# Transformer layers on one NeuronCore: one block per layer instead of three or four, attention started on chunk 0, stack loads on SyncE's queue

## What is computed

```python
x = x + attn_a(layernorm(x))      # gated cumulative attention, once
x = x + ffn(layernorm(x))         # two layers, below
x = x + attn_b(layernorm(x))      # softmax attention, 16 heads of 8, not causal
x = x + ffn(layernorm(x))         # the same two layers again
# ffn: for l in 0, 1:
#   x = x + attn(ln(x)) @ wo + bo                     causal softmax attention, 16 heads of 8
#   h = ln(x)
#   x = x + (token_moe if l == 0 else seq_moe)(h)     top 2 of 8 experts, per token or per sequence
```

## Time and profile before

| | before |
|---|---|
| median of 3 runs | 3304.18 us (3303.13 to 3309.66) |
| the profiled execution | 3296.16 us |
| its span, first to last instruction | 3294.4 us |
| TensorE clock granted, mean | 0.900 of full speed |
| busy: PE, DVE, ACT, POOL | 81%, 78%, 69%, 16% |

### The profile page before, as it was taken

One profiled execution on the slowest core, in us unless ns is written; L12 is line 12 of the kernel. 1 busy time (PEld: TensorE's weight loads), 2 busy tenths in 40 slices (PEclk: granted clock), 3 DMA queues, 4 the chain that ended last, 5 costly groups with the idle time before them and its releaser, 6 DMA issues. The chain is left out here.

```text
span 3294.4 us, 71887 instructions
## 1 busy us (share of the span) xinstructions
PE 2673.7 (81%) x28144; PEld 1180.8 (36%) x28144; DVE 2570.5 (78%) x3323; ACT 2276.4 (69%) x4368; POOL 533.6 (16%) x1036
## 2 busy tenths in 40 slices
PE   4459999599499994759999999289996996699976
PEld 3322332488233332512222222133332784223325
DVE  5659998577498994769999997489995675699956
ACT  1137898377278984539999999168885674488965
POOL 3023110244131001100000000022101342221001
PEclk8669999799599997869999999689997898799988
DMA  1060000121500001140000000510001112300010
GB/s 31 4 146 29 13 10 10 59 60 42 128 21 13 12 10 45 40 90 8 8 10 8 10 8 8 142 34 15 12 10 51 52 49 75 80 16 12 10 37 26
DMA packets 114079, 119.06 MB, mean 36 GB/s; under 512 B 15063, under 2 KB 94733, under 8 KB 113741
## 3 DMA queue, kind: packets, MB, share of 16 engines
q1 hardware_dynamic: 96460, 96.63, 11.1%
q10 hardware_dynamic: 16640, 15.73, 1.9%
q0 software_dynamic: 640, 2.10, 0.3%
HBM read 70.31 MB, written 43.78 MB: 35 GB/s over the span
## 5 line engine op out<-in xcount | busy, mean ns | idle before, releaser
L1185 ACT ACTIVATE h_probsf<-h_ps_scoresf 128x512 f32<-128x512 f32 (+3 forms) x1216 | 603.5, 552 | 157.0 <-PE h_ps_scoresf L1137 144.5
L1185 ACT ACTIVATE h_probsg<-h_ps_scoresg 128x512 f32<-128x512 f32 (+3 forms) x1216 | 603.6, 552 | 151.3 <-PE h_ps_scoresg L1137 138.9
L1185 ACT ACTIVATE h_probsb<-h_ps_scoresb 128x512 f32<-128x512 f32 x1024 | 556.3, 596 | 73.5 <-PE h_ps_scoresb L1137 63.4
L1159 PE MATMUL h_ps_valuesf<-h_probsf,v_all 128*9 128x256 f32 (+2 forms) x4608 | 349.4, 375 | 29.3 <-POOL h_probsf L1248 21.7
L1159 PE MATMUL h_ps_valuesg<-h_probsg,v_all 128*9 128x256 f32 (+2 forms) x4608 | 348.8, 375 | 26.0 <-POOL h_probsg L1248 18.5
L1159 PE MATMUL h_ps_valuesb<-h_probsb,v_all 128*9 128x256 f32 x4096 | 318.4, 383 | 9.4 <-ACT h_drainedb L1192 4.2
L1208 DVE TENSOR_REDUCE h_maxima_0b<-h_ps_scanb 128x2 f32<-128x1024 f32 x256 | 292.5, 1216 | 10.8 <-PE h_ps_scanb L1099 9.9
L1208 DVE TENSOR_REDUCE h_maxima_2b<-h_ps_scanb 128x2 f32<-128x1024 f32 x256 | 292.8, 1217 | 6.7 <-PE h_ps_scanb L1099 6.7
L1208 DVE TENSOR_REDUCE h_maxima_0f<-h_ps_scanf 128x2 f32<-128x1024 f32 x224 | 259.2, 1219 | 22.4 <-PE h_ps_scanf L1099 22.2
L1099 PE MATMUL h_ps_scanf<-k_stack,q_stack 48*128 48x512 bf16 (+3 forms) x1280 | 218.6, 364 | 70.5 <-DVE h_ps_valuesf L1197 51.1
L1099 PE MATMUL h_ps_scang<-k_stack,q_stack 48*128 48x512 bf16 (+3 forms) x1280 | 217.2, 362 | 71.3 <-DVE h_ps_valuesg L1197 51.3
(11 more groups left out here) (404 smaller groups left out, 4287.0 us busy)
## 6 DMA issues: line engine op xcount, KB each, us to landing
q_stack<-combine_weights SPq DMA_DIRECT2D x64, 256.0 KB, 3.2
q_stack<-in_L_ffn_e_w SPq DMA_DIRECT2D x24, 256.0 KB, 2.8
q_stack<-q_parts ACTq DMA_DIRECT2D x20, 256.0 KB, 8.4
k_stack<-k_parts ACTq DMA_DIRECT2D x20, 256.0 KB, 9.9
q_stack<-q_parts SPq DMA_DIRECT2D x20, 256.0 KB, 8.7
k_stack<-k_parts SPq DMA_DIRECT2D x20, 256.0 KB, 10.6
attended<-h_drainedf SPq DMA_DIRECT2D x16, 256.0 KB, 2.2
attended<-h_drainedf SPq DMA_DIRECT2D x32, 128.0 KB, 1.9
```

The costliest lines, as they stand in the source:

```text
L1159: last = nc.tensor.matmul(ps_values[32 * j:32 * j + VD, low:high], m.v_all[:, kb, QUAD * quad + j, :], probs[:, (u + j % banks) % RING_P, ...
L1185: nc.scalar.activation(by_head(probs[:, of % RING_P, :], of), by_head(ps_scores[:, of % RING_S, :], of), ACT.Exp, scale=SOFTMAX_SCALE).the ...
```

## The change

One function, `layer`, now opens one block for a whole layer; the three or four functions write into it, so an engine goes from one to the next as soon as its own semaphores allow. The buffers of attention (`AttentionBuffers`) are allocated before the projection and freed before the experts. What the barriers ordered is now waited for: PE and DVE wait in attention for the projection's last uses of PSUM, SP's and POOL's part of `experts` waits for the end of `finish_attention`. The loads of the stacks move: ACT issues only chunk 0's half b = 1, in its turn for chunk 1 ahead of `copy_chunk(3)`; SP issues all the rest, chunk c - 1's after the high parts of chunk c. The semaphores are cleared at other places. Each block's body is otherwise the same.

```diff
@@ project_qkv: POOL, SP, ACT
-            m.clear_previous(pool)
+            m.clear(pool, "finish", "experts")
...
                     for k in range(2):
                         sp.wait_ge(ready, 2 * c + k + 1)
                         write_part(sp, c, k, part)
-                if c:
-                    load_stacks(sp, c - 1, 0)
+                    if c and part == 0:
+                        load_stacks(sp, c - 1, 0)
+                        if c > 1:
+                            load_stacks(sp, c - 1, 1)
             load_stacks(sp, CHUNKS - 1, 0)
+            load_stacks(sp, CHUNKS - 1, 1)
...
+                if c == 1:
+                    load_stacks(act, 0, 1)
                 if c + 2 < CHUNKS:
                     copy_chunk(c + 2)
...
-                if c:
-                    load_stacks(act, c - 1, 1)
-            load_stacks(act, CHUNKS - 1, 1)
+    return {"h": (h_ready, CHUNKS), "high": (high_ready, 2 * CHUNKS), "rest": (rest_ready, 2 * CHUNKS),
+            "v": (v_kept, CHUNKS)}
@@ attention_heads: PE, DVE, POOL
+            for done in ("h", "high", "rest", "v"):
+                pe.wait_ge(*projected[done])
             pe.wait_ge(cleared, 1)
...
+            dve.wait_ge(*projected["v"])
             nc.vector.memset(ps_values[:, :], 0.0).then_inc(cleared, 1)
...
-            m.clear_previous(pool)
@@ finish_attention
-        @block.gpsimd
-        def _(pool):
-            m.clear_previous(pool)
+        if layer is None:
+            @block.gpsimd
+            def _(pool):
+                pool.wait_ge(added, CHUNKS)
+                m.clear(pool, "project", "attention")
...
+                nc.vector.tensor_tensor(tiles, tiles, ps[:, c, :, :], ALU.add).then_inc(added, 1)
+                dve.wait_ge(added, c + 1)
+                last = chunk_stats(nc, m, dst, c)
+            last.then_inc(measured, 1)
+            dve.wait_ge(measured, 1)
...
+    return projected
@@ experts: POOL, SP
-            m.clear_previous(pool)
             inverse_root(nc, pool, m, m.rstd[:, :], tmp[:, 0, :], var_ready, rstd_ready, 1)
+            if by_token:
+                pool.wait_ge(hn_ready, CHUNKS)
             for e in range(n_exp):
                 pool.wait_ge(w2_in[e], 16)
...
                 pool.wait_ge(evacuated, y + 1)
+                if y == CLEAR_AT:
+                    m.clear(pool, "project", "attention", "finish")
...
+            sp.wait_ge(attended, CHUNKS)
             if by_token:
@@ new
+CLEAR_AT = 4
+def layer(nc, m, n, number=None, first=False, last=False, load_experts=False, out=None):
+    mixing = number is None
+    with nc.Block() as m.block, ExitStack() as ctx:
+        buffers = AttentionBuffers(nc, ctx, n, not mixing, load_experts)
+        projected = project_qkv(nc, m, n, first=first, layer=number)
+        attention_heads(nc, m, n, buffers, projected)
+        attended = finish_attention(nc, m, n, number)
+        ctx.close()
+        if not mixing:
+            experts(nc, m, n, number, last, attended, out)
```

More of the change, by code:

```diff
@@ L77, with phase_semaphores @@
 class Memory:
-    def phase_semaphores(self):
-        self.previous, self.current = self.current, []
+    def phase_semaphores(self, phase):
+        here = self.used[phase] = []
         def sem(name):
@@ L86, in sem, with clear @@
                 self.named[name] = self.ctx.enter_context(self.nc.semaphore(name))
-            self.current.append(self.named[name])
+            here.append(self.named[name])
             return self.named[name]
         return sem
-    def clear_previous(self, pool):
-        for s in self.previous:
-            pool.sem_clear(s)
+    def clear(self, pool, *phases):
+        for phase in phases:
+            for s in self.used.pop(phase, ()):
+                pool.sem_clear(s)
     def __init__(self, nc, ctx, ins):
-        self.nc, self.ctx, self.named, self.current, self.previous = nc, ctx, {}, [], []
+        self.nc, self.ctx, self.named, self.used, self.block = nc, ctx, {}, {}, None
         def sb(name, shape, dt=F32):
@@ L305, in chunk_stats @@
     for t in range(c * TPC, (c + 1) * TPC):
-        nc.vector.bn_stats(m.st[:, t, :], src[:, t, :])
+        last = nc.vector.bn_stats(m.st[:, t, :], src[:, t, :])
+    return last
 def token_stats(nc, step, m, tmp, var_ready, rstd_ready, count):
@@ L1049, in attention_heads @@
     with ExitStack() as ctx:
[L1050 to L1060, removed]
-        raw_weights = sb("h_raw_weights", [P, 2, FF]) if load_experts else None
+        sem = m.phase_semaphores("attention")
         ps_scan = ctx.enter_context(nc.psum_tensor("h_ps_scan" + n, [P, RING_A, 2, SCAN_KEYS], F32))
@@ L1070, in attention_heads @@
         out_done = [sem(f"h_out_done{k}") for k in range(2)]
-        block = ctx.enter_context(nc.Block())
+        block = m.block
         def by_head(bank, u):
@@ L1286, in sb @@
             return ctx.enter_context(nc.sbuf_tensor(name + n, shape, dt))
-        sem = m.phase_semaphores()
+        sem = m.phase_semaphores("finish")
         y = sb("f_y", [P, CHUNKS, CH])
@@ L1317, in _ @@
         def _(dve):
-            step = Steps(dve, dve_steps)
             dve.wait_ge(sums_in, 16)
@@ L1385, with experts @@
 CW_AT, TURN_BACK_AT = 8, 8
-def experts(nc, m, n, layer, last, out=None):
+CLEAR_AT = 4
+def experts(nc, m, n, layer, last, attended, out=None):
     by_token = layer == 0
@@ L1396, in sb @@
             return ctx.enter_context(nc.sbuf_tensor(name + n, shape, dt))
-        sem = m.phase_semaphores()
+        sem = m.phase_semaphores("experts")
         tmp = sb("e_tmp", [P, 3, TILES])
@@ L1811, in _ @@
                     sp.wait_ge(written, 16 * CHUNKS)
-def feed_forward(nc, m, n, load_experts=False, out=None):
-    for layer in range(LAYERS):
-        tag = f"{n}{layer}"
-        project_qkv(nc, m, tag, first=layer == 0, layer=layer)
-        attention_heads(nc, m, tag, causal=True, load_experts=load_experts and layer == 0)
-        finish_attention(nc, m, tag, layer)
-        experts(nc, m, tag, layer, last=layer == LAYERS - 1, out=out if layer == LAYERS - 1 else None)
+def layer(nc, m, n, number=None, first=False, last=False, load_experts=False, out=None):
[8 more added lines that the diff above has]
+            experts(nc, m, n, number, last, attended, out)
+def feed_forward(nc, m, n, load_experts=False, out=None):
+    for number in range(LAYERS):
+        last = number == LAYERS - 1
+        layer(nc, m, f"{n}{number}", number, first=number == 0, last=last,
+              load_experts=load_experts and number == 0, out=out if last else None)
 def build(nc, ins, out):
@@ L1831, in build @@
         feed_forward(nc, m, "f", load_experts=True)
-        project_qkv(nc, m, "b", layer=None)
-        attention_heads(nc, m, "b", causal=False)
-        finish_attention(nc, m, "b")
+        layer(nc, m, "b")
         feed_forward(nc, m, "g", out=out)
```

41 lines of the change are left out of this document (27 added, 14 removed).

## The result

The changed kernel took **3321.82 us** (median of 7 runs, 3318.53 to 3326.54) against 3304.18 us (7 runs of the kernel before). The ratio is **1.0058, 95% interval 1.0041 to 1.0076**: slower by 0.6%. I had forecast 3280 us, in a range of 3262 to 3301, with a chance of 0.07 for slower.

A forecast was written before the change was run, and what follows sets the result against it. It took PE's idle time at the barrier before attention's first search, with the stacks' DMA traffic behind it, as the bound. Terms -20 + 1.2 - 4 - 2.2 - 1.0 + 1.6 = -24.4 us gave 3279.8 us, range 3262 to 3301.

The forecast's parts named there:

- main term: Projection to attention, four causal layers: without the barrier, scores start at 896.6 instead of 901.62, 5.0 us faster a layer.
- Rival 1: Stack loads in f1: one queue carries them less well, 185 GB/s, last load 7.9 us later, 3319 us; chance 0.09.
- The rest of the seam: Projection to attention, causal layers: search starts near 870, stops after some 13 us; PE idles 13 us or more for the shift.
- Rival 4: Causal layers: scores start 18 us early because the shift doesn't wait, 3226 us; chance 0.03.
- Layer b: Search there needs chunk 3's keys: loads start 0.6 us earlier, 1.8 lost at the gate, 1.2 us slower.
- POOL's splits: Weight splits in f0 and g0 move behind DVE's normalisations, with some blocking beside choose: net 4 us faster for both.
- The small seams: Attention to finish and finish to experts, without their barriers: 2.2 us and 1.0 us faster.
- Attention to finish: Five times, SP goes on at once after the last result without the barrier: 0.45 us each, 2.2 us faster.
- Finish to experts: Four times, DVE's barrier of 0.30 us becomes a wait on measured of 0.05: 1.0 us faster.
- The clearing at the end of b: POOL clears 33 semaphores after the last addition, 2.5 us, so the barrier comes 1.6 us later.

The follow-up runs named there:

- experiment 2: Kernel after, SP's queue still alone with the loads of chunks 1 to 3, but issued behind the low parts of the next chunk, not the high: 3303.1 us.
- experiment 10: experiment 6 with ACT's loads of chunk 0 moved earlier, behind the high parts of chunk 1 as in the kernel after: 3244.2 us.
- experiment 1: Kernel after, stack loads put back on both queues in the kernel before's places (ACT behind middle parts, SP behind low parts): 3280.8 us.
- experiment 9: Kernel after, with the four loads of chunk 3, b = 1, issued by ACT instead of SP: 3309.8 us.
- experiment 5: Kernel after, with the two DMAs of shift(0) in the four causal layers issued on POOL's queue instead of SP's: 3286.1 us.
- experiment 4: Kernel before with one line of the change: POOL waits for the last normalised chunk before splitting weights in f0 and g0: 3295.0 us.
- experiment 6: experiment 1 with shift(0) of the causal layers issued on POOL's queue instead of SP's: 3251.8 us.
- experiment 8: experiment 1 with all stack loads on ACT's queue, chunk c - 1 behind the middle parts of chunk c, and part writes on SP's: 3270.5 us.

## Why the prediction was wrong, point by point

**The step that failed** is the first of the main term: "The bytes are the same; at the rate of the earlier trace rows they take 40.4 us", and with it "At the first two later gates the high parts of the next chunk are still queued and keep the DMA engines fed". I took a rate that two queues had reached and gave it to one. Measured: 50.9 us instead of 42.2. Of the 10.5 us over my 40.4, about 7 are the queue (experiment 2: 47.9 us with no holes, against 40.9 in experiment 10 with the same bytes on two queues) and 3 the place (50.9 against 47.9), where I had put 1.8. Nor were the bytes the same: the early start takes in 9.5 MB instead of 8.9, which cost nothing in f1 (experiment 10: 40.9 us), but some 2.3 us on the mean of the five layers (42.6 against 40.3 in experiment 1). The last writes that a gate waits for now stand behind the loads before them on the same queue, up to eight. At 865.78 the last of them had just landed and the two high parts behind them were in by 867.4, before the first new load landed at 869.6; so each of the three gates opens onto engines that run empty, where I counted one hole of 1.8 us. The term of -5.0 us became +2.7 in f1.

**Rival 1 was what happened**, with its place and nearly its price: it put the last load 7.9 us late at 185 GB/s and the kernel at 3319. Measured: 186 GB/s over the stretch, the last load 8.7 us later than forecast, 3321.8 us. That its numbers fit so well is partly luck: the stretch holds 9.5 MB and not 8.9, and the 186 GB/s have the holes of the place in them, which the rival did not have; without the holes one queue carried 198 (experiment 2). I gave it 0.09, because "the DMA share is already full with two queues". A full share says that the engines are occupied, not how much they move: at 1.12 it was 195 GB/s of loads with both queues and 155 with one (experiment 9 and the kernel after). The last stretch of the earlier trace rows, 0.94 at 170 GB/s, was no hint of that, though I used it as a bound: it ran on two queues, and its rate is low because it holds loads alone and the end, where the share falls. From 887 to 896 the kernel before moved 189 GB/s of loads at 1.12, and the 221 of the whole stretch have the faster writes in them. No row of before showed what one queue does.
The Trainium skill (DMA: Bandwidth & Descriptors, "Issuing engines are not separate DMA queues") says that DMAs started by several engines interleave on the same 16 engines and that a second issuer saves only the sequencer's time. Experiment 9 disagrees for these loads: with the same bytes, and with issue faster than landing on one queue too, the second queue took 2.2 us off 12.3.

**The rest of the seam was right.** The shift sets the scores, not the search; the search starts at 870 and stops 12 us later; PE waited over 13 us (21.9). Experiment 1 gives the term its due: with the loads left on both queues the scores of f1 come 4.3 us earlier than before, close to the 5.0 that I had put down, and the kernel takes 3280.8 us. My number was right for a change that this one is not, and its parts less so: of the 5.0 us I had put 1.5 on an earlier last landing, which came 0.2 later there, so that the whole gain is the barrier's. Rival 4 was rightly held back by SP's order, which the kernel after shows with its 21.9 us of waiting. But "I know no way around it" was too narrow: experiment 5 went round SP's order, by another queue, and took 35 us off the kernel after by the ratios.

**Layer b**: forecast 1.2 us slower, measured 9.5, since here the landing of the last load counts in full; the bound was 7.

**POOL's splits**: -4 forecast, -5.8 by the medians in experiment 4 (interval by the ratios 4.3 to 11.6, 4.7 in the two profiles). L1527 takes 4.4 us for 10.7, and blocked steps show in `choose`. Timelines of DVE and POOL, f0, kernel after:

```profile
638.75 1.27 POOL L1495 TENSOR_TENSOR e_w_lof<-q_stack,e_w_hif 128x512 fp32r<-128x512 f32 x1
...
638.86 1.32 DVE L1383 SCALAR_TENSOR_TENSOR q_stack<-q_stack 128x128 f32<-128x128 f32 x1
```

This operation of DVE, with two SBUF inputs, took 1.32 us in place of 0.29 and ended 0.16 us behind POOL's subtraction. The page SBUF — State Buffer of the Trainium skill ("SBUF: two separate sides") has it so: the one that comes second is blocked until the first is done. But only two steps of 13 were held in full, and `choose` took 6.3 us for 4.0: the blocking is 2.3 us in f0 and 1.6 in g0, where I took 1.5, and the term doesn't vanish, as the page alone would have had it.

**The small seams** were each priced too high. Attention to finish: in f1 2.14 us lie between SP's last write and the first sums read, for 2.37: 0.23 a layer, not 0.45. Finish to experts: DVE waits 0.24 us for its own statistics, where the barrier took 0.30; I had taken 0.05. Together about 1.4 us instead of 3.2. The clearing at the end of b cost 1.8 us, forecast 1.6; timeline of DVE, start of g0:

```profile
2095.86 0.19 DVE L288 TENSOR_TENSOR p_tmpg<-st 128x16 f32<-128x16 f32 x1 [2.08 <-PEq L1847]
```

**g0** (+7.2 us in its seam) is partly the profile of before, not the change: there its loads began 15.6 us behind the transpose and its scores at 59.2, while in experiment 4, with the same projection, they began at 18.2 and 62.3. So about 3 of the 26.5 us are chance of one profile, in line with the 17.6 us by the medians against 25.2 by the spans.

## What to carry to other kernels

A rate read from a trace belongs to the queues that produced it: before loads are gathered on one queue, look for a stretch where one queue alone carried them, and if there is none, price the loss. On one queue, don't put the writes that the next gate waits for behind the loads of this one: issue the writes first, then the loads. And when a barrier goes, the next thing late is often a small DMA at the end of a long queue; giving that one DMA a queue of its own was worth 27 us here by the ratios (experiment 6 against 1), more than all that the change gains without its loads (20, experiment 1).

## What the runs showed of the hardware that I had not expected

- Two queues carry the same eight loads faster than one when nothing else is under way: 10.1 us against 12.3 to the last landing, though both start at about 4 us. Why the engines, at a full share, move less from one queue was not tried.
- What they move at a full share depends still more on what it is. Where the part writes land it was 338 GB/s with both queues (experiment 1, 871 to 876 us, share 1.10) and 344 with one (experiment 2, 872 to 876, share 1.10). Where loads alone were left it was 183 and 170 (878 to 888, share 1.14; 879 to 891, share 1.15). So two windows can be compared by their rate only if they hold the same kind of DMA.
- A shift of two DMAs of 2 KB lands in 3.0 to 4.1 us on a queue of its own when a gate had just opened (share 0.67), in 6.9 to 7.8 with loads queued on two other queues, and in 11 at the end of a queue that holds loads (issued at 879.18, in by 890.45, experiment 1). In experiment 8 it took up to 10.6 us behind part writes on its queue, with a full queue of loads beside it. A queue of one's own spares the issue order, and only part of the wait.
